# VectorE's order in the expert stage of a decoder layer: the gate-times-up product ahead of the small PSUM banks while slot tiles run

## The reference

```python
xn = layernorm(x) * ln_gamma + ln_beta                       # 1024 x 128
probs = softmax(xn @ router_w)                               # 8 experts
topv, topi = top_k(probs, 2); topv = topv / sum(topv)
comb = sum(one_hot(topi, 8) * topv[..., None], axis=1)
swiglu(x, gu, dn): gate, up = split(x @ gu); gate = clip(gate, -10, 10)
                   return (silu(gate) * up) @ dn             # 128 -> 2 x 512 -> 128
out = sum_e comb[:, e] * swiglu(xn, gate_up_w[e], down_w[e]) + swiglu(xn, shared_gate_up_w, shared_down_w)
x = layernorm(x + out)
```

## Time and profile before

| what | value |
|---|---|
| median of 3 runs | 1805.33 us (1801.79 to 1805.59) |
| the profiled execution, its own time | 1805.96 us |
| its span in the trace | 1803.9 us |
| PE, DVE, ACT, POOL busy over the span | 96%, 82%, 61%, 15% |
| mean granted TensorE clock | 0.989 of full |
| first clip of the expert stage (unit 0) | 1663.2 us |
| clip of unit 30 | 1751.1 us |
| last clip (unit 48) | 1789.4 us |

### The profile page before, as it was taken

The page is one execution under the profiler, slowest core; times in us unless marked ns, Lnnn a source line. Parts: engine busy times, 40 slices in busy tenths (PEclk is TensorE's granted clock), DMA queues, the critical chain, the costliest instruction groups (busy, mean ns, idle before and its releaser), DMA issues.

```text
span 1803.9 us, 31501 instructions
## 1 busy us (share of the span) xinstructions
PE 1730.7 (96%) x9280; PEld 867.8 (48%) x9280; DVE 1484.8 (82%) x2398; ACT 1105.7 (61%) x1355; POOL 265.3 (15%) x344
## 2 busy tenths in 40 slices
PE   6977999999999999999999999999999999999897
PEld 4854444444444444444444444444444444445664
DVE  7968988888888888888879797978788888776777
ACT  4554666666666666666666666666666666676454
POOL 4746992000000000000000000000000000002344
PEclk8989999999999999999999999999999999999999
DMA  5001210000000000000000000000000000001000
GB/s 166 2 1 35 70 41 1 0 0 0 0 0 0 0 0 0 0 0 0 0 0 0 0 0 0 0 0 0 0 0 0 0 0 1 0 1 35 2 2 13
DMA packets 17753, 16.68 MB, mean 9 GB/s; under 512 B 6047, under 2 KB 15907, under 8 KB 17318
## 3 DMA queue, kind: packets, MB, share of 16 engines
q1 hardware_dynamic: 17446, 15.48, 2.8%
q0 software_dynamic: 256, 0.53, 0.1%
HBM read 13.95 MB, written 2.06 MB: 9 GB/s over the span
## 4 chain that ended last, share of the span: by engine, by line
PE 88%; DVE 5%; ACT 3%; issue 3%; POOL 0%; DMA 0%; DVEq 0%; SPq 0%; POOLq 0%; ACTq 0%
PE PS L1727 88%; ACT p_arena L930 1%; DVE mxs L1582 1%; DVE mxs L1318 1%; ACT p_arena L923 0%; DVE z_arena L1615 0%; DVE w_arena L1099 0%; DVE w_arena L1273 0%; DVE acc L1620 0%; ACT z_arena L766 0%; POOL w_arena L586 0%; PE PS L1736 0%; DMA vecs<-in_L_attn_b_conv_w 0%; POOL z_arena L714 0%; DVE z_arena L1606 0%
## 5 line engine op out<-in xcount | busy, mean ns | idle before, releaser
L920 ACT ACTIVATE p_arena<-PS 128x1024 f16<-128x1024 f32 (+1 forms) x480 | 484.4, 1009 | 527.9 <-PE PS L1727 527.7
L1727 PE MATMUL PS<-a_arena,z_arena 128*128 (+1 forms) x2832 | 746.2, 379 | 4.5 <-DVE a_arena L1337 4.1
L1727 PE MATMUL PS<-p_arena,z_arena 128*128 128x512 f16 x2800 | 740.5, 379 | 1.4 <-ACT p_arena L930 0.3
L1318 DVE TENSOR_REDUCE mxs<-PS 128x512 f32 (+1 forms) x900 | 582.5, 668 | 91.0 <-PE PS L1727 87.8
L1350 DVE TENSOR_TENSOR p_arena<-p_arena 128x1024 f16<-128x1024 f32 (+1 forms) x480 | 574.5, 1197 | 96.3 <-ACT p_arena L923 89.3
L923 ACT ACTIVATE p_arena<-PS 128x1024 f32<-128x1024 f32 (+1 forms) x480 | 482.0, 1004 | 0.0
L1727 PEld LDWEIGHTS PS<-a_arena,z_arena 128*128 (+1 forms) x2832 | 274.8, 98 | 331.8 <-DVE a_arena L1337 4.4
L1727 PEld LDWEIGHTS PS<-p_arena,z_arena 128*128 128x128 f16 (+1 forms) x2800 | 269.3, 98 | 311.7 <-ACT p_arena L930 8.8
L1727 PE MATMUL PS<-z_arena,a_arena 128*128 (+3 forms) x1024 | 353.6, 361 | 10.5 <-DVE mxs L1318 8.2
L698 POOL IOTA a_arena<- 128x512 f16 x1 | 0.6, 557 | 1289.8 <-DVE acc L1361 1289.8
L1727 PEld LDWEIGHTS PS<-z_arena,a_arena 128*128 (+1 forms) x1024 | 97.8, 98 | 144.0 <-DVE mxs L1318 26.5
(11 more groups left out here) (324 smaller groups left out, 1015.1 us busy)
## 6 DMA issues: line engine op xcount, KB each, us to landing
w_arena<-in_L_ffn_gate_up_w SPq DMA_DIRECT2D x8, 512.0 KB, 3.6
p_arena<-in_ctx SPq DMA_DIRECT2D x2, 1600.0 KB, 9.2
w_arena<-in_L_ffn_down_w SPq DMA_DIRECT2D x8, 256.0 KB, 4.0
a_arena<-in_L_xattn_Wkv SPq DMA_DIRECT2D x1, 1024.0 KB, 5.9
xg_dram<-VO SPq DMA_DIRECT2D x1, 975.0 KB, 8.6
w_arena<-in_x SPq DMA_DIRECT2D x1, 512.0 KB, 4.2
a_arena<-in_L_xattn_Wo SPq DMA_DIRECT2D x1, 512.0 KB, 6.9
w_arena<-in_L_xattn_Wq SPq DMA_DIRECT2D x1, 512.0 KB
```

The lines of the kernel that those rows point to most:

```text
L920: s.activation(Phi[:, r % 3, 0:w], ps, ACT.Exp, scale=1 / SSC).then_inc(hi_ready, 1)
L1318: v.tensor_reduce(mxs[:, i, bass.ds(kb, 1)], PS[:, 6 + par, 0:w], AX.X, ALU.max).then_inc(mx_read, 1)
L1727: return t.matmul(o, l, r, start=start, stop=stop)
```

## The change

In the steps 1 to 29 VectorE takes the product of the unit before right behind the clip, and the small banks behind that. Steps 30 to 48 keep the order of before. No instruction is added or taken away, no semaphore, buffer or bank changes, and the other engines' programs are the same.

```diff
             for u in range(NUNITS):
                 clip(u)
-                if u:
+                if 0 < u < COMB_END:
+                    hidden(u - 1)
+                    for kind, a, t in work_at(u - 1, 0) + work_at(u - 1, 1):
+                        small_dve(kind, a, t)
+                elif u:
                     for kind, a, t in work_at(u - 1, 0) + work_at(u - 1, 1):
                         small_dve(kind, a, t)
                     hidden(u - 1)
```

## The result

The changed kernel took 1812.44 us in the median of 6 runs (1809.73 to 1813.93), the kernel before 1803.86 in 6 (1801.79 to 1806.31). The ratio is 1.0042 with a 95% interval of 1.0029 to 1.0054. Measured again beside later experiments it was 1811.63 us with a ratio of 1.0037 (1.0024 to 1.0050). The forecast was 1807.3 us, no change that can be told; the time lies outside its range of 1803.0 to 1810.0. The 94 times of the kernel before that were taken beside this and the later kernels fall into two groups, 36 near 1802.2 us and 58 near 1806.4, so its median moves from series to series (1803.86, 1806.27, 1804.97, 1806.08), and a kernel is compared by its ratio to the runs taken beside it, not by its median.

What follows compares the result with a forecast made beforehand. The chain of waits, 88% TensorE, was taken as the bound. Terms 1.8 + 0.1 + 0.2 - 1.4 - 0.4 + 1.9 - 0.2 gave +2.0 us; from median 1805.33, forecast 1807.3, range 1803.0 to 1810.0.

Steps and rivals of the forecast that it cites:

- Part a: Steps 4 to 6: the product stands inside three closed loops of gate, clip and y, 0.60 us each, +1.8 us.
- Rival three: Steps 4 to 6: TensorE's longer idle time brings a further stretch at 1.2 GHz, up to 1.7 us, 1809.0 us; chance 0.09.
- Rival two: Steps 7 to 9: GpSimd's earlier subtraction delays VectorE's L1412 and norm rows (L1279), +2.9, 1810.2 us; chance 0.12.
- Part b: Step 10: product costs +0.60, the selection no longer slowed beside GpSimd gives -0.54, together +0.1 us.
- Part c: Steps 12 and 13: a wait for the product goes, but a bank for turned rows comes 0.60 later; +0.2 us.
- Parts d and e: Steps 14 to 17: chain to GpSimd's remainder 1.4 us earlier, -1.4; a quarter of the following 1.2 GHz loss gone, -0.4.
- rival one: Moved-forward products win, the half-rate stretch goes whole (-1.7), only one late tie holds: -1.2, 1804.1 us; chance 0.2.
- Part f: Late ties just met before: step 19 +0.2, step 20 +0.6, step 21 +0.5, step 28 +0.6, together +1.9 us.
- Part g: Step 30: the up product's wait for the product (L1615) shrinks, -0.2 us.

Runs made afterwards that it cites:

- TensorE kept busy: The changed kernel with six thrown-away matmuls of 512 columns ahead of TensorE's waits in steps 4, 5 and 6: 1808.60 us, ratio 1.0021 to the kernel before.
- both remedies: The changed kernel with norm rows ahead of small banks in steps 3, 8, 9 and six matmuls ahead of TensorE's waits in steps 4 to 6: 1804.63 us, ratio 1.0002.

## Why the prediction was wrong, step by step

The forecast of +2.0 knew the mechanisms and left two of them out of its sum. In the changed kernel, stretch by stretch:

| stretch | forecast | measured | what made it |
|---|---|---|---|
| clip 0 to 4 | 0 | +0.88 | norm rows of step 3 |
| clip 4 to 7 | +1.8 | +3.57 | three products, and 6.8 us more at 1.2 GHz |
| clip 7 to 10 | 0 | +1.32 | norm rows of steps 8 and 9 |
| clip 10 to 11 | +0.1 | +1.24 | a new stretch at 1.2 GHz; 0.06 with TensorE kept busy |
| clip 11 to 17 | +0.2 | +0.06 | |
| clip 17 to 18 | -1.8 | -2.63 | the wait for GpSimd, and its stretch at 1.2 GHz |
| clip 18 to 30 | +1.9 | +2.01 | waits of steps 20, 21, 28, and L1441 |

The three cuts measured +4.27 (steps 4 to 6), +2.10 (steps 3, 8, 9) and -0.57 (the rest) over the stage, together +5.80 of +6.45. They do not add up clip by clip: at clip 7 their sum is 1.67 above the changed kernel, since two of them have more time at 1.2 GHz in the same steps, and from clip 10 to 11 the changed kernel loses the 1.24 that none of the cuts has.

- **Part a, the first mis-sized term.** Forecast +1.8, bounded at 2.0, with the words "with 0.68 each it would be 2.0". Measured +3.57 from clip 4 to 7 in the changed kernel, 3.6 to 4.1 in the four traces that have this order and no added matmuls. The waits grew by 0.60 each, as said, and without any stretch at 1.2 GHz the three cost 1.85. The bound failed because it priced the wait and not the clock behind it. Rival three had this at 0.09 chance and "up to 1.7"; it should have been a term of the sum. The rows were there: the only stretch at 1.2 GHz between clip 0 and 1700 us lay in these steps before the change.
- **Rival two, which belonged in the sum.** It was given 0.12 and priced at 2.9, and the sum had nothing for it. It came true in its second half, the norm rows: 2.20 us in the changed kernel. Its first half, L1412, did not happen. The failed step is the weighing. By the rival's own times, rows that start 1.7 to 1.8 us behind a clip and need 0.6 to 1.1 us cannot be through at 2.01, so that the rows would meet GpSimd was certain, and only for L1412 was it a matter of 0.09 us. Who would then wait was not certain: in step 3 before they met as well, and GpSimd waited. The prediction treated them as one event, and it overlooked the four rows of step 3.
- **Part b.** The selection took 0.34 us, as said. In step 9 it was relieved too (0.78 before, 0.35 after), but the norm rows behind it took more than that back. With both remedies clip 10 to 11 grew by 0.17, near the +0.1.
- **Part c.** Forecast +0.2. In the cut without steps 3 to 6, 8 and 9, clip 11 to 14 moved by 0.07: right within its bounds.
- **Parts d and e.** Forecast -1.8 together, measured -2.62 from clip 17 to 18 in that cut and -2.63 in the changed kernel. The wait for GpSimd fell to 0.9, against 0.8 forecast. The stretch at 1.2 GHz went whole, which rival one had and the quarter taken in part e did not.
- **Part f.** Forecast +1.9, measured +1.89 from clip 18 to 30 in that cut. The three ties named for steps 20, 21 and 28 came, at about 0.6 each. The exact number is luck: step 18 gave 0.71 by a collision that nobody had named (L1441), and from clip 19 to 20 it gained 0.42.
- **Part g.** Forecast -0.2, measured -0.09, behind clip 30.
- **What was left out.** The measured medians lie 8.6 us apart, the two profiled executions 3.8, and the stage gives 6.45. Most of what is between them lies ahead of clip 0, which came 2.5 us earlier in the profile of the changed kernel and moves with the clock of the program's first part. Clip 0 comes at 1659.4 with 23.9 us at 1.2 GHz in the first 300 us of the trace, at 1660.7 to 1660.8 with 27.3, and at 1663.3 to 1664.2 with 34.1 (with 30.7 anywhere from 1660.5 to 1663.8). The prediction took 1805.33 from three runs; six gave 1803.86. Whether the changed kernel's first part was slower on the whole stays open.

Both signs that the prediction had named for its slower rivals were there: L1279 of more than 1 us, and further stretches at 1.2 GHz before 1700.

The Trainium skill's rule on the shared ports ("SBUF — State Buffer", section "Who interferes with whom": whoever comes first holds the pair for its whole instruction) was named in the prediction for either side. The trace agrees with it on L1412, which came 0.10 us first, and on GpSimd's 1.60 us there. On the norm rows it agrees that one of the two waits out the other, but who came first can't be read off the recorded starts, which in steps 8 and 9 lie 0.04 us apart with the waiting row ahead.

## What to carry to other kernels

An engine that is fed earlier starts its own work earlier: ask what that work runs into, and check each instruction of the neighbour separately, by its distance from a common event, and not the group as one chance. Where TensorE is idle in each turn of a closed loop and the trace already shows a stretch at 1.2 GHz there, price a longer wait at more than its length: here 1.8 us of added waits cost 3.6 to 4.1. And cut an order by steps before judging it: a single step held the gain (2.77 us of the stage, ratio 0.9981), and with the other 28 beside it the stage ended at +6.45. Look too at how far the clips move where nothing was changed up to there, here by up to 0.5 us, before the steps of a cut are weighed.

## What the runs showed of the hardware

- A GpSimd subtraction of 1.16 us that started 0.29 us behind the first of two norm rows made the second wait until it was over (1.53 instead of 0.59 us for the two). The wait is recorded inside the row's duration, 1.28 instead of 0.34 us.
- A VectorE instruction on 32 columns lost nearly as much beside GpSimd as the norm rows of 128: L1441 0.90 instead of 0.18 us, L1437 1.04 instead of 0.18.
- Eighteen matmuls whose results are thrown away made a kernel's stage 3.48 us shorter: TensorE stayed at 2.4 GHz through the stage, where it had stood at 1.2 GHz for 13.7 us.
- Where the stretches at 1.2 GHz fall differs between traces of unchanged steps: steps 1 to 6 in the old order had 3.4 us of it in three traces and none in a fourth.
- Two profiles of the changed kernel agree on each collision to 0.01 us, and on clip 0 to 30 to 0.25 us, while whole runs of one kernel differ by 4 to 6 us.
